# Graph network kernel on one core: the maximum subtracted by TensorE, some one-hots by VectorE, own logits moved into the maxima's loads, row statistics by chunk

## The reference, cut to what matters

```python
def _gatv2_layer(x, src, dst, Wl, bl, Wr, br, att, bias, heads, out_ch, concat):
    xl = (x @ Wl + bl).reshape(N, heads, out_ch)
    xr = (x @ Wr + br).reshape(N, heads, out_ch)
    e = jax.nn.leaky_relu(xl[src] + xr[dst], NEG_SLOPE)
    logits = jnp.einsum('ehc,hc->eh', e, att)
    m = jax.ops.segment_max(logits, dst, num_segments=N)
    ex = jnp.exp(logits - m[dst])
    denom = jax.ops.segment_sum(ex, dst, num_segments=N)
    alpha = ex / denom[dst]
    msg = xl[src] * alpha[..., None]
    out = jax.ops.segment_sum(msg, dst, num_segments=N)
...
x = x + _L0_gnn_ref(h, ...)                 # two such layers and a dense one
h = jnp.maximum(_layernorm(x, axis=-1), 0.0)
...
h = jnp.maximum(_layernorm(x, axis=-1), 0.0)
x = x + _L3_gnn_ref(h, ...)                 # three graph convolutions
```

## Time and profile before

| | |
|---|---|
| median of 3 runs | 6864.06 us (6855.04 to 6872.8) |
| the profiled execution | 6867.52 us, span 6865.7 us |
| PE, POOL, DVE, ACT busy | 82%, 68%, 55%, 31% of the span |
| mean granted clock of PE | 0.93 of 2.4 GHz |

### The profile page before, as it was taken

The page is one execution under the profiler, slowest core; times in us unless marked ns, Lnnn a source line. Parts: engine busy times, 40 slices in busy tenths (PEclk is TensorE's granted clock), DMA queues, the critical chain, the costliest instruction groups (busy, mean ns, idle before and its releaser), DMA issues. The chain is left out here.

```text
span 6865.7 us, 123063 instructions
## 1 busy us (share of the span) xinstructions
PE 5634.3 (82%) x35774; PEld 4549.4 (66%) x35774; DVE 3765.0 (55%) x12913; ACT 2158.0 (31%) x6967; POOL 4656.2 (68%) x4393
## 2 busy tenths in 40 slices
PE   2799999647769999985886996666666499999999
PEld 2688888546668777774775996666666355555555
DVE  6655552289975555322887445666666544344343
ACT  4233334259833333333994003222222310000000
POOL 1777777678877777777887661777777157376473
PEclk8899999779969999996997998999999799999999
DMA  5788875756634444335554884555555389999998
GB/s 198 236 283 281 277 211 159 124 108 141 139 58 105 105 103 104 84 81 49 76 76 122 289 288 139 158 157 160 158 157 158 32 291 305 300 303 301 301 305 262
DMA packets 904054, 1232.19 MB, mean 179 GB/s; under 512 B 230602, under 2 KB 640862, under 8 KB 890408
## 3 DMA queue, kind: packets, MB, share of 16 engines
q1 hardware_dynamic: 607544, 887.00, 40.4%
q0 software_dynamic: 207392, 219.55, 18.4%
q10 hardware_dynamic: 88428, 117.57, 5.0%
HBM read 987.45 MB, written 237.38 MB: 178 GB/s over the span
## 5 line engine op out<-in xcount | busy, mean ns | idle before, releaser
L1023 POOL DMA_INDIRECT ACC<-table,TABS x1760 | 1722.4, 979 | 586.7 <-issue 578.2
L1348 POOL DMA_INDIRECT BUF<-table,TABS x840 | 796.9, 949 | 615.6 <-DMA table<-ACC 260.6
L1107 POOL DMA_INDIRECT adjacency<-TABS x600 | 993.0, 1655 | 264.1 <-issue 210.2
L1023 POOL DMA_INDIRECT BUF<-table,TABS x880 | 838.1, 952 | 331.5 <-issue 331.5
L1809 PE MATMUL picked<-ident,ACC 128*128 128x128 f32 (+1 forms) x3520 | 714.1, 286 | 0.0
L2158 PE MATMUL asum<-BUF 128*128 128x144 f32 x3520 | 566.1, 306 | 164.8 <-DVE BUF L2136 160.4
L1885 DVE SCALAR_TENSOR_TENSOR BUF<-BUF,TABS,wspread 128x128 bf16<-128x128 f32 (+1 forms) x600 | 324.2, 540 | 624.0 <-issue 610.1
L2158 PEld LDWEIGHTS asum<-BUF 128*128 128x128 f32 x3520 | 480.6, 199 | 195.7 <-issue 181.5
L1808 PE MATMUL picked<-G,OH 128*128 128x128 f32 (+1 forms) x2352 | 498.7, 296 | 119.3 <-DVE G L1785 60.7
L2104 ACT ACTIVATE BUF<-iota_row,TABS 128x128 f32<-128x128 f32 x1760 | 555.2, 386 | 101.3 <-PEq L89 101.3
L1802 PE MATMUL picked<-ident 128*128 128x128 f32 x3520 | 560.0, 307 | 11.1 <-PEq L89 11.1
(11 more groups left out here) (408 smaller groups left out, 10913.4 us busy)
## 6 DMA issues: line engine op xcount, KB each, us to landing
TABS<-adjacency SPq DMA_DIRECT2D x272, 512.0 KB
BUF<-in_edge_pair SPq DMA_DIRECT2D x880, 128.0 KB
BUF<-adjacency SPq DMA_DIRECT2D x102, 1024.0 KB
BUF<-adjacency SPq DMA_DIRECT2D x204, 512.0 KB
adjacency<-zeros ACTq DMA_DIRECT2D x44, 1792.0 KB
G<-adjacency SPq DMA_DIRECT2D x136, 512.0 KB
kept<-ACC SPq DMA_DIRECT2D x220, 272.0 KB, 2.8
G<-kept SPq DMA_DIRECT2D x220, 272.0 KB
```

Source lines behind the costliest of these rows:

```text
L1023: po.indirect_dma_start(rows[:, slot, j, 0:width], None, tab, bass.IndirectOffsetOnAxis(ap=SRC[:, q * GT + j:q * GT + j + 1], axis=0)).the ...
L1107: po.indirect_dma_start(adj_flat, bass.IndirectOffsetOnAxis(ap=PLACE[:, k:k + 1], axis=0), TOTAL[:, k:k + 1], None, compute_op=ALU.add).th ...
L1348: po.indirect_dma_start(R[:, q % deep_ring, j, :], None, table, bass.IndirectOffsetOnAxis(ap=SRC[:, k:k + 1], axis=0)).then_inc(S(f"gather ...
```

## The change

- `gat_sums`: `less_max` is gone from DVE. PE makes the difference itself in a new buffer `dif`: the logits times the identity, plus the maxima times `MINUS` (minus the identity), added up in PSUM. `exps` reads `dif` there. The fourth one-hot of a group is made by DVE, in every fourth group of layer 1 and in every group of layer 2 (`last_hot`). The second buffer pair takes two more PSUM banks.
- `edge_max` takes the own logits (`own_logits`), in three parts in layer 1 and one in layer 2, in room beside the first penalties; the loads of the second penalties wait for them. `gat_logits` starts without them.
- `add_back` takes the statistics of each block's rows (`bn_stats`) after its chunk; `mean_and_root` joins them by operations of 49 columns; `stage` subtracts and scales from `X` itself by a `tensor_scalar` per block, and ACT cuts at zero while it copies. SP no longer waits for `staged` before it loads into the room of the centred copy.

```diff
--- before.py
+++ after.py
@@ -666,17 +666,18 @@
             end()
 
 
-        def centre(src, dst, tmp):
-
-            mean, var = st[0][:, 0:NB], st[1][:, 0:NB]
-            go(ve, lambda: ve.tensor_reduce(mean, src, AX_X, ALU.add))
-            go(ve, lambda: ve.tensor_scalar(mean, mean, 1.0 / D, None, ALU.mult))
-            go(ve, lambda: ve.tensor_tensor(dst, src, tall(mean), ALU.subtract))
-            go(ac, lambda: ac.activation(tmp, dst, ACT.Square))
-            go(ve, lambda: ve.tensor_reduce(var, tmp, AX_X, ALU.add))
-            go(ve, lambda: ve.tensor_scalar(var, var, 1.0 / D, EPS, ALU.mult, ALU.add))
-            inv_sqrt(var, var)
-            return var
+        def mean_and_root(halves, less_mean, root):
+
+            (mean_a, sum_a), (mean_b, sum_b) = ((halves[:, :, 3 * i + 1], halves[:, :, 3 * i + 2]) for i in range(2))
+            apart = st[4][:, 0:NB]
+            go(ve, lambda: ve.tensor_tensor(less_mean, mean_a, mean_b, ALU.add))
+            go(ve, lambda: ve.tensor_scalar(less_mean, less_mean, -0.5, None, ALU.mult))
+            go(ve, lambda: ve.tensor_tensor(apart, mean_a, mean_b, ALU.subtract))
+            go(ve, lambda: ve.scalar_tensor_tensor(apart, apart, 0.25, apart, ALU.mult, ALU.mult))
+            go(ve, lambda: ve.tensor_tensor(root, sum_a, sum_b, ALU.add))
+            go(ve, lambda: ve.scalar_tensor_tensor(root, root, 1.0 / D, apart, ALU.mult, ALU.add))
+            go(ve, lambda: ve.tensor_scalar(root, root, EPS, None, ALU.add))
+            inv_sqrt(root, root)
 
         def inv_sqrt(dst, src):
 
...
@@ -1438,8 +1436,11 @@
                 def stage(c):
                     blocks, at, cols = chunk(c)
                     wait(ve, S("turned"), c - 1)
-                    ve.scalar_tensor_tensor(T[c % 2][:, 0:blocks * P].rearrange("p (b d) -> p b d", b=blocks), B0[:, at, :],
-                                            0.0, tall(rstd[:, at]), ALU.max, ALU.mult).then_inc(S("staged"), 1)
+                    for j in range(blocks):
+                        b = at.start + j
+                        m = ve.tensor_scalar(T[c % 2][:, j * P:(j + 1) * P], Xn[:, b, :], less_mean[:, b:b + 1],
+                                             rstd[:, b:b + 1], ALU.add, ALU.mult)
+                    m.then_inc(S("staged"), 1)
 
                 def move(p, k):
 
...
@@ -1531,7 +1532,7 @@
                     cols = chunk(c)[0] * P
                     ac.wait_ge(S("turned"), c + 1)
                     wait(ac, S("hidden"), c - 1)
-                    ac.activation(XT[:, c % 2, 0:cols], turned[c % 2][:, 0:cols], ACT.Copy).then_inc(S("copied"), 1)
+                    ac.activation(XT[:, c % 2, 0:cols], turned[c % 2][:, 0:cols], ACT.Relu).then_inc(S("copied"), 1)
 
                 def copy_hidden(c):
...
@@ -1754,13 +1755,6 @@
             XRB = [OH[:, 0, :, 0:W], OH[:, 1, :, 0:W], tail.rearrange("p (t w) -> p t w", t=GT)]
 
 
-            Zn = area[:, :, 0:W]
-            meanwhile(None, 0, [
-                lambda: ve.tensor_tensor(Zn, XL, XR, ALU.add),
-                lambda: ve.scalar_tensor_tensor(Zn, Zn, SLOPE, Zn, ALU.mult, ALU.max),
-                lambda: ve.tensor_tensor(Zn, Zn, wide(att[:, 0:W]), ALU.mult),
-                lambda: ve.tensor_reduce(self_l, Zn.rearrange("p b (h c) -> p b h c", h=H), AX_X, ALU.add)])
-            sp.wait_ge(S("between"), 4)
             with ExitStack() as ps:
                 picked = [psum(ps, f"picked{i}", [P, GT * P]) for i in range(4)]
...
@@ -1965,6 +1959,21 @@
             begin()
 
             in_dram = head_d[0:P * L].rearrange("(c n) -> c n", c=P)
+            W = H * C
+            beside = BUF[2][:, :, :].rearrange("p b d -> p (b d)")[:, L // 2:]
+            parts = -(-NB * W // beside.shape[1])
+
+            def own_logits():
+
+                most = -(-NB // parts)
+                for low in range(0, NB, most):
+                    at = slice(low, min(NB, low + most))
+                    n = at.stop - low
+                    z = beside[:, 0:n * W].rearrange("p (b w) -> p b w", b=n)
+                    go(ve, lambda: ve.tensor_tensor(z, XL[:, at, :], XR[:, at, :], ALU.add))
+                    go(ve, lambda: ve.scalar_tensor_tensor(z, z, SLOPE, z, ALU.mult, ALU.max))
+                    go(ve, lambda: ve.tensor_tensor(z, z, wide(att[:, 0:W], n), ALU.mult))
+                    go(ve, lambda: ve.tensor_reduce(self_l[:, at, :], z.rearrange("p b (h c) -> p b h c", h=H), AX_X, ALU.add))
             HALVES = [slice(0, L // 2), slice(L // 2, L)]
             sums_of_pens = [ends[:, 4 + i:5 + i] for i in range(4)]
 
...
@@ -1979,6 +1988,7 @@
                                      open_d[0:TILES * P].rearrange("(c n) -> c n", c=chunks)[:, cols]
                                      ).then_inc(S(f"opens{i}"), 16)
                 ac.wait_ge(S("opens0"), 16 * H)
+                ac.wait_ge(chain[0].sem, chain[0].n)
                 for h in range(H):
                     ac.dma_start(closes[h * chunks:(h + 1) * chunks, :],
...
@@ -2062,17 +2073,24 @@
             HOT = BUF[2][:, at:at + RING * GT, :].rearrange("p (r t) d -> p r t d", r=RING)
             at += RING * GT
             MX = BUF[2][0:TH, at:at + RING, :]
-            DIF = BUF[2][:, at + RING:at + 2 * RING, 0:TH].rearrange("p r (t h) -> p r t h", h=H)
+            MINUS = BUF[2][0:TH, at + RING, 0:TH]
+
+            def by_scalar(q):
+
+                return GT - 1 if H == 1 or q % 4 == 3 else GT
+
+            early = [sum(by_scalar(i) < GT for i in range(q + 1)) for q in range(GROUPS)]
             by_group = head_d[0:H * TILES * P].rearrange("(h g t e) -> g t h e", h=H, t=GT, e=P)
             whole, R, LOGIT = ring(W, H)
             with ExitStack() as ps:
                 mcol = [psum(ps, f"mcol{i}", [P, 4 * P]) for i in range(2)]
+                dif = [psum(ps, f"dif{i}", [P, 4 * P]) for i in range(2)]
                 sums = [psum(ps, f"asum{i}", [P, GT, 2 * P]) for i in range(2)]
                 adder = Adder(acc, sums, WA, "summed")
 
                 def fetch_max(q, slot, turn):
 
-                    wait(sp, S("mcol"), q - RING + 1)
+                    wait(sp, S("dif"), q - RING + 1)
                     settle(sp, "sync")
                     if H == 1:
...
@@ -2090,8 +2108,15 @@
                 def turn_max(q, slot, turn):
                     pe.wait_ge(S(f"max{slot}"), 16 * (1 if H == 1 else GT) * (turn + 1))
                     wait(pe, S("mfirst"), q - 1)
-                    m = pe.matmul(mcol[slot % 2][:, 0:TH], MX[:, slot, :], ident[0:TH, 0:TH], start=True, stop=True)
-                    m.then_inc(S("mcol"), 1)
+                    wait(pe, S("exp"), q - 1)
+                    pe.matmul(mcol[slot % 2][:, 0:TH], MX[:, slot, :], ident[0:TH, 0:TH], start=True, stop=True
+                              ).then_inc(S("mcol"), 1)
+                    if q == 0:
+                        pe.wait_ge(S("minus"), 1)
+                    pe.wait_ge(S(f"got{slot}"), 16 * (turn + 1))
+                    less = dif[slot % 2][:, 0:TH]
+                    pe.matmul(less, ident[:, :], LOGIT[:, slot, :], start=True, stop=False)
+                    pe.matmul(less, MX[:, slot, :], MINUS, start=False, stop=True).then_inc(S("dif"), 1)
 
                 def by_head(a):
                     return a.rearrange("p (t h) -> p t h", h=H)
...
@@ -2100,31 +2125,32 @@
 
 
                     wait(ac, S("summed"), q - RING + 1)
-                    for j in range(GT):
-                        ac.activation(HOT[:, slot, j, :], iota_row[:, :], ACT.Abs, scale=-1.0,
-                                      bias=LOCAL[:, bass.ds(q * GT + j, 1)]).then_inc(S("gap"), 1)
+                    for j in range(by_scalar(q)):
+                        m = ac.activation(HOT[:, slot, j, :], iota_row[:, :], ACT.Abs, scale=-1.0,
+                                          bias=LOCAL[:, bass.ds(q * GT + j, 1)])
+                    m.then_inc(S("gap"), 1)
+
+                def last_hot(q, slot, turn):
+
+                    if by_scalar(q) < GT:
+                        wait(ve, S("summed"), q - RING + 1)
+                        one_hot(HOT[:, slot], q * GT, GT - 1).then_inc(S("last_hot"), 1)
 
                 def exps(q, slot, turn):
                     ac.wait_ge(S("dif"), q + 1)
-                    ac.activation(RHS[:, slot, :, W:W + H], DIF[:, slot], ACT.Exp).then_inc(S("exp"), 1)
-                    ac.wait_ge(S("gap"), (q + 1) * GT)
-                    ac.activation(HOT[:, slot], HOT[:, slot], ACT.Relu, scale=-1.0, bias=1.0
-                                  ).then_inc(S("hot"), 1)
+                    ac.activation(RHS[:, slot, :, W:W + H], by_head(dif[slot % 2][:, 0:TH]), ACT.Exp
+                                  ).then_inc(S("exp"), 1)
+                    ac.wait_ge(S("gap"), q + 1)
+                    tiles = HOT[:, slot, 0:by_scalar(q), :]
+                    ac.activation(tiles, tiles, ACT.Relu, scale=-1.0, bias=1.0).then_inc(S("hot"), 1)
 
```

(40 more changed lines are left out.)

6 lines of the change are left out of this document (2 added, 4 removed).

## The result

The changed kernel took 7646.99 us (median of 4 runs, 7643.54 to 7652.15), the kernel before 6860.78 us beside it: ratio 1.1144, 95% interval 1.1125 to 1.1163. It is 786 us slower; 7650 us was forecast. The profiled execution took 7643.54 us, its span is 7641.7 us, 776 us longer than that of before.

The account below looks back on a forecast made before the run. POOL bounds the logits stages and its merges nearly end the sums stages; changed, PE at 1.2 GHz would bound the sums. +813 - 12 - 14 = +787 us gives 7651, say 7650 us; range 7550 to 7730.

Parts of the forecast that it names:

- The sum: Whole kernel: clock +813, own logits -12, statistics -14, together +787 us.
- The clock: Both sums stages: small `dif` passes keep PE at 1.2 GHz throughout; +388, +419 and +6 for drains, +813 us.
- the lower bound from the earlier trace: Sums stages: least price of a small two-pass product, with neighbours of its shape, 0.43 us at 1.2 GHz.
- The first: Rival, sums stages: clock rises to 2.4 GHz despite small passes; 2.32 us a group, 6986 us in all; chance 0.1.
- the rule that the prediction held against itself: Sums stages: the Trainium skill says sustained matmul activity releases the throttled clock, so an always busy PE runs at 2.4 GHz.
- The second: Rival, sums stages: PE's idle time swallows the new passes at 2.4 GHz, both under 0.30 us; 6827 us; chance 0.06.
- The third: Rival, sums stages: one stage recovers the clock and the other doesn't; about 7320 us; chance 0.03.
- The waits of PE: Sums stages: PE's added waits for the exponential two groups back and the kept rows cost nothing.
- The own logits: Moved from logits to maxima stages: -23 us from freed POOL, +6 layer 1, +5 layer 2, net -12 us.
- The statistics: `centre` mostly replaced, -24.5 us, against 49 `bn_stats` at 0.22 us, some 10.5 us; net -14 us.

Follow-up runs that it names:

- e1_narrow: Kernel before plus two unread narrow products on PE per group of both sums stages (32 columns in layer 1, 4 in layer 2): 9016.12 against 8374.91 us, ratio 1.0770.
- e2_wide: Kernel before plus four unread PE passes of 128 columns per group of both sums stages: 8391.31 against 8374.91 us, ratio 1.0032.
- e4_asum224: Changed kernel with the sums' products padded to 224 columns in place of 144, both layers: 8670.55 us against 8374.91 for the kernel before, ratio 1.0361.
- e8_warm: Changed kernel with 40 unread PE products of 128 columns ahead of each sums stage: 9223.73 us (one execution), kernel before 8437.32, changed kernel 9215.52.
- e9_joined: Changed kernel with `mcol` and the maxima's part of `dif` in one product, `first_max` waiting for the exponential: 8945.78 us, ratio 1.0596 to the kernel before.
- e10_joined_warm: e9_joined with the run-up of e8_warm (unread PE products before the sums): median 8508.03 us of ten executions, 8392 to 8805; kernel before 8436.35.
- e12: e10_joined_warm with layer 1's sums padded to 160 columns: 6829.24 us against 6864.01 for the kernel before, ratio 0.9953.
- e6_rest: Kernel before with only the own logits moved and the statistics by chunk, `gat_sums` as before: 8411.54 against 8437.32 us, ratio 0.9971.
- e3_dve_max: Changed kernel with `less_max` on DVE again and `dif` gone from PE: 8387.24 us against 8374.91 for the kernel before, ratio 1.0015.

## Why the prediction was right

**The sum.** The close total, +787 forecast and +786 measured in the medians, is partly luck. The two traces differ by 776 us: the clock's term is 5 us too large, the statistics' 2 too small a gain, and block 2 has 5.7 us that no term had. The medians lie 10 us further apart than the profiled executions. The range of 7550 to 7730 did not need that luck.

**The clock, +813.** Measured +388.0 and +419.6, +808. The price of a small product, 0.56 and 0.51 us by the `mcol` of the earlier trace rows, was right to the hundredth in the changed kernel, where the number of rows alternates as it does around `mcol`; in e1_narrow, where it alternates less, two of the three cost 0.40 and 0.45, close to the lower bound from the earlier trace rows. The step on which all rested, that small passes in a loop that starts at 1.2 GHz keep it there, is shown: narrow passes bring the loss (e1_narrow), wide ones in the same number don't (e2_wide), and widening the sums takes most of it away (e4_asum224). My reason in the text, that the stage "starts at 1.2 GHz and nothing in it ever makes the loop denser", was half of it: e8_warm loses the clock from above as well. The two halves meet in layer 2 of e9_joined and e10_joined_warm: the joined loop keeps 2.4 GHz if it starts there, and never reaches it if it starts at 1.2. In layer 1 it kept it to the end only in e12, with 160 columns and on another chip.

**The rivals.** The first, and the rule that the prediction held against itself for it, fail on the windows: PE is busy without a gap for 850 and 810 us, at 0.50. It took 2.32 us a group for a loop at 2.4 GHz; e8_warm shows 2.18, a small product costing 0.34 us and not 0.39. At that price, 477 us a stage, it would have been some 6925 us and not 6986. The second turned at 0.30 us for both products together; they cost 0.68 at 2.4 GHz. The third needed one stage to recover; both stayed at 0.50, on two chips.

**The waits of PE, nothing.** Right: in the changed kernel PE waits 1.5 us in all before the sums and 3.9 us for loads of the kept rows, and e4_asum224 and e12_joined_warm160, which have the same waits, run at PE's or POOL's pace.

**The own logits, -12.** Measured -18.9, +7.6, -5.7 and +5.0, net -12.0. The first gathers and, in layer 2, the merges beside the four operations (start, length):

```profile
173.00 0.95 POOL L1024 DMA_INDIRECT ACC<-table,TABS  x1 [47.58 <-issue]
174.25 0.96 POOL L1024 DMA_INDIRECT ACC<-table,TABS  x1 [0.30 <-issue]
...
3540.81 3.43 DVE L1973 TENSOR_TENSOR BUF<-BUF 128x3136 f32<-128x3136 f32 x1 [12.62 <-PEq L89]
3541.83 3.83 POOL L1108 DMA_INDIRECT adjacency<-TABS  x1 [9.89 <-issue]
3544.27 3.42 DVE L1974 SCALAR_TENSOR_TENSOR BUF<-BUF 128x3136 f32<-128x3136 f32 x1
3545.97 3.17 POOL L1108 DMA_INDIRECT adjacency<-TABS  x1 [0.30 <-issue]
3547.73 3.42 DVE L1975 TENSOR_TENSOR BUF<-BUF,att 128x3136 f32<-128x3136 f32 x1
3549.44 3.14 POOL L1108 DMA_INDIRECT adjacency<-TABS  x1 [0.30 <-issue]
3551.19 3.42 DVE L1976 TENSOR_REDUCE st<-BUF 128x49 f32<-128x3136 f32 x1
3552.89 1.57 POOL L1108 DMA_INDIRECT adjacency<-TABS  x1 [0.30 <-issue]
```

A merge alone takes 1.57 us. Three merges are held up by 5.4 us in all, the stage by 5.0. The fourth, beside the reduction, isn't. The Trainium skill (SBUF — State Buffer, "Who interferes with whom") says that a DVE instruction with two SBUF inputs contends with a GpSimd instruction that reads SBUF, and that `tensor_reduce` never does; the trace agrees for both. It says there too that the second operand is what takes the shared read interface; no run here shows that.

**The statistics, -14.** Measured +8.0 and -23.9, net -15.9; e6_rest, with these two parts alone, has 26 us less on its chip, against 28 by the terms. Of `bn_stats` a row of the trace now has the price:

```profile
L2727 DVE BATCH_NORM_STATS2 st<-X x49: 274/277/295, 6242.0 to 6259.5; 128x6 f32<-128x128 f32 x49
6258.44 0.87 DVE L2727 BATCH_NORM_STATS2 st<-X 128x6 f32<-128x128 f32 x4
```

0.28 us for one, but they overlap: four take 0.87 us, 0.22 each, the value taken. A little more of them than forecast lay under other work.

**Left open.** Block 2, whose code is unchanged, is 5.7 us shorter; no term had that, and no run was made for it. It may be no more than what two executions differ by.

**What I had wrong behind the prediction.** That the loss would be as large with any small pass (e1_narrow, 170 us less than expected), that a one-hot on DVE is nearly free (e3_dve_max), that layer 2 would fall first in e8_warm (it kept 2.4 GHz longer), and that a loop at 2.4 GHz either holds or falls at once (e10_joined_warm). What makes it fall in one group and not in another stays open.

## What to carry to other kernels

Before giving PE more work because it has idle time, look at its granted clock in that stage and at how dense its wide passes are: small products cost more than their length when they thin the loop out. Here they held PE at 1.2 GHz, where the sums of a group take 2.22 us in place of 1.15. Where a loop must carry them, join them, start it with the clock up, and try wider padding, which in e4_asum224 gave back far more than it cost. Time several executions: those of e10_joined_warm lie 412 us apart. Then look at which engine ends the stage, for here POOL's merges leave no more than some 10 us to win. Read a term of a sum from a row with the same neighbours, not from a row with the same operation only.
